# Layer 1's input groups in a two-layer adaLN transformer kernel: normalised one slot later and transposed in mid-slot; joined epsilon and power steps; no carrier copies

## What is computed

```
h = _layernorm(x) * (1 + ca) + sa;  x = x + ga * attention(h)
h = _layernorm(x) * (1 + cb) + sb;  x = x + gb * ffn(h)
```

## Time and profile before

| | us |
|---|---|
| median of 3 runs | 736.52 |
| the profiled execution's own time | 740.21 |
| its span, first to last instruction | 738.4 |
| PE busy (88%) | 647.3 |
| DVE busy (69%) | 511.4 |
| ACT busy (43%) | 319.5 |
| POOL busy (30%) | 222.5 |
| PE idle until `xn` of L1320 was ready, whole span (13 times, at most 3.6) | 18.0 |
| DVE, L1320, 112 tiles | 41.4 |
| DVE, L1203, 98 copies | 15.0 |

### The profile page before, as it was taken

The page is one execution under the profiler, slowest core; times in us unless marked ns, Lnnn a source line. Parts: engine busy times, 40 slices in busy tenths (PEclk is TensorE's granted clock), DMA queues, the critical chain, the costliest instruction groups (busy, mean ns, idle before and its releaser), DMA issues.

```text
span 738.4 us, 11039 instructions
## 1 busy us (share of the span) xinstructions
PE 647.3 (88%) x3816; PEld 504.9 (68%) x3828; DVE 511.4 (69%) x1465; ACT 319.5 (43%) x644; POOL 222.5 (30%) x225
## 2 busy tenths in 40 slices
PE   5889799988777999988889989958889998799997
PEld 4456687877556778775678777846677786576674
DVE  5957598696768667726669777596865754876665
ACT  1133344445234454543344444523445453554453
POOL 3333654343545211004455435253421102000000
PEclk9989999999879999999999999978999999999999
DMA  8400000000000000000000000000000000000001
GB/s 262 110 0 1 2 1 1 1 0 1 1 0 1 1 1 1 1 1 1 1 1 1 1 1 2 1 1 0 1 1 1 1 1 1 0 16 29 14 19 40
DMA packets 12078, 9.64 MB, mean 13 GB/s; under 512 B 1708, under 2 KB 10744, under 8 KB 12024
## 3 DMA queue, kind: packets, MB, share of 16 engines
q1 hardware_dynamic: 12024, 8.94, 4.1%
HBM read 6.84 MB, written 2.10 MB: 12 GB/s over the span
## 4 chain that ended last, share of the span: by engine, by line
PE 69%; DVE 18%; ACT 5%; POOL 4%; issue 4%; DMA 1%; SPq 0%; ACTq 0%; POOLq 0%
PE ps L777 14%; PE ps L647 12%; PE ps L755 8%; PE ps L606 5%; DVE xn L1320 5%; PE ps L922 4%; PE ps L924 4%; PE ps L923 4%; PE ps L800 3%; PE ps L665 2%; PE ps L801 2%; PE ps L595 2%; PE ps L816 2%; DVE row_max L1357 1%; PE ps L601 1%
## 5 line engine op out<-in xcount | busy, mean ns | idle before, releaser
L1083 ACT ACTIVATE probsT<-ps 128x512 f32<-128x512 f32 (+3 forms) x160 | 85.2, 533 | 180.4 <-PE ps L755 180.4
L777 PE MATMUL ps<-v_sb,probsT 128*128 128x129 f32 (+1 forms) x1148 | 157.1, 280 | 3.7 <-ACT probsT L1085 3.7
L777 PEld LDWEIGHTS ps<-v_sb,probsT 128*128 128x128 f32 (+1 forms) x1148 | 141.5, 191 | 10.6 <-ACT probsT L1085 5.5
L1357 DVE TENSOR_REDUCE row_max<-ps 128x1 f32<-128x512 f32 (+2 forms) x144 | 87.6, 619 | 48.3 <-PE ps L647 18.1
L755 PE MATMUL ps<-ident,probs 128*128 128x128 f32 (+1 forms) x574 | 95.7, 285 | 16.7 <-ACT probsT L1083 6.0
L755 PEld LDWEIGHTS ps<-ident,probs 128*128 128x128 f32 (+1 forms) x574 | 67.5, 143 | 49.0 <-issue 45.3
L1057 ACT ACTIVATE probs<-ps,neg_max 128x512 f32<-128x512 f32 (+7 forms) x158 | 92.8, 618 | 16.9 <-DVE neg_max L1364 16.0
L473 POOL TENSOR_TENSOR rstd<-veps,half 128x4 f32<-128x4 f32 x34 | 34.2, 1012 | 154.1 <-DVE veps L1211 153.9
L501 POOL TENSOR_TENSOR hq<-ha,hp 128x352 f32<-128x352 f32 x32 | 29.9, 934 | 139.5 <-DVE hp L1398 139.5
L647 PE MATMUL ps<-k_high,q_high 128*128 128x512 f32 (+4 forms) x112 | 46.0, 411 | 0.6 <-ACT probs L1005 0.6
L1152 ACT ACTIVATE probs<-ps 128x512 f32<-128x512 f32 x40 | 24.0, 599 | 44.7 <-PE ps L924 44.7
(11 more groups left out here) (240 smaller groups left out, 1380.8 us busy)
## 6 DMA issues: line engine op xcount, KB each, us to landing
out<-x_sb SPq DMA_DIRECT2D x8, 256.0 KB, 2.3
x_sb<-in_L_attn_x SPq DMA_DIRECT2D x2, 512.0 KB, 5.3
hT_all<-in_L_wmod SPq DMA_DIRECT2D x2, 384.0 KB
rope_cos<-table_cos SPq DMA_DIRECT2D x1, 768.0 KB, 7.5
rope_sin<-table_sin SPq DMA_DIRECT2D x1, 768.0 KB, 9.1
rope_cos<-table_cos SPq DMA_DIRECT2D x1, 256.0 KB, 4.1
rope_sin<-table_sin SPq DMA_DIRECT2D x1, 256.0 KB, 5.1
moe_raw<-in_L_ffn_expert_gate_w SPq DMA_DIRECT2D x1, 256.0 KB, 4.2
```

Source lines behind the costliest of these rows:

```text
L777: mm = pe.matmul(bank(OUT_AT, 0, V_W), probsT[0:size, n % 4, k * P:(k + 1) * P], v_sb[0:size, j, :], start=(c == 0 and k == 0), stop=(c == ...
L1083: ins = act.activation(probsT[:, n % 4, 0:full], bank(TURN, 0, full), ACT.Copy)
L1357: ins = dve.tensor_reduce(dst, ps[:, start:start + width], AX.X, ALU.max, negate=single)
```

## The change

1. norm2 leaves `input_turns` and `normalise_in_slot`. Group g is normalised in slot 4g + 13 instead of 4g + 12, on DVE between the first maximum and `combine` (`normalise_keys`), and transposed in mid-slot on PE, behind the second scores; ACT copies it behind `copy_hq`.
2. Where norm1 or norm3 and norm2 end in one slot (slots 11, 15, 19, 23), eight `bn_aggr` follow each other, and one epsilon and one power of 128x8 replace two of 128x4. The semaphores per kind are merged accordingly.
3. `carry_wait` is gone: the waits stand on the instructions behind it.

```diff
-    firsts = (("fp4_in", FFN_LAG), ("norm2", DOWN_LAG + GROUP + 1), ("norm3", TILES + GROUP + 2))
+    firsts = (("fp4_in", FFN_LAG), ("norm3", TILES + GROUP + 2))
...
+def key_group(slot):
+
+    return group_at(slot, DOWN_LAG + GROUP + 1)
...
-                    if at(NORM1_SLOT) is not None:
-                        rsqrt(0, at(NORM1_SLOT))
-                    if at(NORM2_SLOT) is not None:
-                        rsqrt(1, at(NORM2_SLOT))
+                    if s % GROUP == GROUP - 1:
+                        rsqrt(0, 1 + (at(NORM2_SLOT) is not None), b * 2 * GROUPS + s // GROUP + 1)
...
                         if c + 1 < following:
                             scores(s + 1, c + 1)
+                        if c == 0 and key_group(s) is not None:
+                            turn_group(("norm2", key_group(s)))
...
                             copy_hq(s - DOWN_LAG)
+                        if c == 0 and key_group(s) is not None:
+                            copy_group(("norm2", key_group(s)))
...
-            def carry_wait():
-
-                dve.tensor_copy(tick[:], ones[:, 0:1])
-
-            def send_statistics(kind, link):
-
-                carry_wait()
-                for k in range(GROUP):
-                    ins = dve.bn_aggr(mv[:, kind, k, :], bn[:, kind, k, :])
+            def send_statistics(kind, kinds, link):
+
+                for n in range(kind, kind + kinds):
+                    for k in range(GROUP):
+                        ins = dve.bn_aggr(mv[:, n, k, :], bn[:, n, k, :])
                 link(ins)
-                dve.tensor_scalar(veps[:, kind, :], mv[:, kind, :, 1], LN_EPS, None, ALU.add).then_inc(var_ready[kind], 1)
+                rows = slice(kind, kind + kinds)
+                dve.tensor_scalar(veps[:, rows, :], mv[:, rows, :, 1], LN_EPS, None, ALU.add).then_inc(var_ready[kind // 2], 1)
...
-                    if at(NORM2_SLOT) is not None:
-                        normalise(1, at(NORM2_SLOT), at(NORM2_SLOT)).then_inc(xn_ready, 1)
...
+                def normalise_keys(g):
+
+                    normalise(1, GROUPS // 2 + g, g).then_inc(xn_ready, 1)
...
                     if following:
                         maximum(s + 1, 0)
+                    if key_group(s) is not None:
+                        normalise_keys(key_group(s))
```

More of the change, by code:

```diff
@@ L140, in turn_order @@
                 order.append(("hq", s - DOWN_LAG))
+            if c == 0 and key_group(s) is not None:
+                order.append(("norm2", key_group(s)))
     return order + [("norm3", GROUPS - 1)]
@@ L154 @@
 ROPE_SUMS = 2 * (GROUPS - 1)
-NORM_GROUPS = (2 * GROUPS, GROUPS, GROUPS)
+NORM_GROUPS = (2 * GROUPS, 2 * GROUPS, GROUPS)
 parts_before, MAX_PARTS = before(lambda l, i: len(score_chunks(l, i)) if len(score_chunks(l, i)) > 1 else 0)
-STEPS_PER_BATCH = 185
+STEPS_PER_BATCH = 177
 def build(nc, x, cos, sin, wq, wk, wv, w_gate, w_up, w_down, c0, wmod0, qk, ov, gate_w, lb_bias,
@@ L204, in build @@
         unpick = sb("unpick", [P, PAIRS, P], BF16)
-        half = sb("half", [P, GROUP])
+        half = sb("half", [P, 2, GROUP])
         priority = sb("priority", [P, EXPERTS])
@@ L326, in build @@
         tanh_ready = sem("tanh_ready")
-        var_ready = [sem(f"var_ready_{k}") for k in range(3)]
-        rstd_ready = [sem(f"rstd_ready_{k}") for k in range(3)]
+        var_ready = [sem(f"var_ready_{k}") for k in ("inner", "first")]
+        rstd_ready = [sem(f"rstd_ready_{k}") for k in ("inner", "first")]
         xn1_ready = sem("xn1_ready")
@@ L468, in _, with rsqrt @@
             pool.tensor_copy(ident_b[:], ident[:]).then_inc(consts, 1)
[L470 to L476, removed]
+            def rsqrt(kind, kinds, n):
+                rows = slice(kind, kind + kinds)
+                pool.wait_ge(var_ready[kind // 2], n)
+                pool.tensor_tensor(rstd[:, rows, :], veps[:, rows, :], half[:, 0:kinds, :],
+                                   ALU.pow).then_inc(rstd_ready[kind // 2], 1)
+            rsqrt(2, 1, 1)
+            rsqrt(2, 1, 2)
             pool.wait_ge(fp4_scaled, 1)
@@ L484, in _ @@
             for b in range(BATCH):
-                def rsqrt(kind, n):
-                    rsqrt_at(kind, b * NORM_GROUPS[kind] + n + 1)
                 def modulate_1(g):
@@ L554, in _ @@
                     if early_group(s, NORM0_SLOT) is not None:
-                        rsqrt(2, early_group(s, NORM0_SLOT))
+                        rsqrt(2, 1, b * GROUPS + early_group(s, NORM0_SLOT) + 1)
                     if s in (NEXT_SLOT - 2, NEXT_SLOT):
-                        rsqrt(2, GROUPS + (s == NEXT_SLOT))
-                    if at(NORM1_SLOT) is not None:
-                        rsqrt(0, at(NORM1_SLOT))
-                    if at(NORM2_SLOT) is not None:
-                        rsqrt(1, at(NORM2_SLOT))
+                        rsqrt(2, 1, (b + 1) * GROUPS + (s == NEXT_SLOT) + 1)
+                    if s % GROUP == GROUP - 1:
+                        rsqrt(0, 1 + (at(NORM2_SLOT) is not None), b * 2 * GROUPS + s // GROUP + 1)
                     if at(NORM2_SLOT + 2) is not None:
                         keys_low(at(NORM2_SLOT + 2))
-                    if at(NORM3_SLOT) is not None:
-                        rsqrt(0, GROUPS + at(NORM3_SLOT))
                     if at(FP4_SLOT) is not None:
@@ L1221, in first_statistics @@
                 link(ins)
-                send_statistics(2, link)
+                send_statistics(2, 1, link)
             def first_normalise(b, batch, g):
-                dve.wait_ge(rstd_ready[2], (b + 1) * GROUPS + g + 1)
+                dve.wait_ge(rstd_ready[1], (b + 1) * GROUPS + g + 1)
                 for t in range(GROUP):
@@ L1306, in x_tile, with statistics @@
                     return x_sb[:, bass.ds(b * TILES + t, n), :].rearrange("p t d -> p (t d)")
[L1308 to L1314, removed]
+                def statistics(kind, t):
+                    return dve.bn_stats(bn[:, kind, t % GROUP, :], x_tile(t))
                 def normalise(kind, n, g):
-                    dve.wait_ge(rstd_ready[kind], b * NORM_GROUPS[kind] + n + 1)
+                    dve.wait_ge(rstd_ready[kind // 2], b * NORM_GROUPS[kind] + n + 1)
                     for t in range(GROUP):
@@ L1346, in norm_0_statistics @@
                 def norm_0_statistics(g):
-                    statistics(2, range(g * GROUP, (g + 1) * GROUP))
+                    for t in range(g * GROUP, (g + 1) * GROUP):
+                        ins = statistics(2, t)
+                    link(ins)
+                    send_statistics(2, 1, link)
                 def maximum(s, c):
@@ L1377, in finish @@
                     dve.wait_ge(x_attn, b * SLOTS + s + 1)
-                    carry_wait()
-                    statistics(0, [i])
+                    ins = statistics(0, i)
                     if ffn_tile(s, DOWN_LAG) is not None:
-                        statistics(1, [s - DOWN_LAG])
+                        ins = statistics(1, s - DOWN_LAG)
+                    if s % GROUP == GROUP - 1:
+                        link(ins)
+                        send_statistics(0, 1 + (ffn_tile(s, DOWN_LAG) is not None), link)
                 def quantise(a, m, src, n_blocks, scales, last_wait):
```

## The result

The kernel with the change took **760.21 us** (median of 4 runs, 758.13 to 762.10) against 736.65 us before (4 runs): ratio 1.0313, 95% interval 1.0273 to 1.0352. It is slower by 23.6 us, where 14.2 us were forecast, and lies above the range of 735 to 757.

The account below looks back on a forecast made before the run. PE's work, 69% of the chain, was taken to set the time except where PE waits for DVE. Terms of 5.8 + 1.1 + 0 + 1.0 - 1.8 + 1.0 = 7.1 us a batch, 14.2 for two, gave 750.7 us, range 735 to 757.

Parts of the forecast that it names:

- The sign and the mechanism: Slower: DVE reaches norm2's tiles late, beside POOL's work, so PE stands in mid-slot; chance of slower 0.77.
- slot 13 to L757: Slot 13: PE waits for late tiles, then bare ACT copies, and goes on later: +5.8 us a batch, undisturbed +1.7.
- slot 17: Tiles beside `xq_scaled` free `TURN` at 209.8 for next slot's L696, which ran at 208.66: +1.1 us, undisturbed -2.9.
- slot 25, to L757: Slot 25, POOL quiet: tiles can no longer be done while PE is in the slot before: +1.0 us.
- The DVE chain of slot 13: DVE's maximum done at 158.1, `xq_scaled` on POOL from 157.6, four tiles ready at 161.8.
- the clock's term: Slot 13: PE's stand three times as long, restart at lower clock: +1.0 us a batch, between 0 and 3.
- a deeper clock loss: Rival: PE stays at 1.2 GHz for the rest of slots 13 and 21: +3 a batch, 755 us; chance 0.14.
- My 0 for slot 21: Slot 21: tiles beside `hq_scaled`, transposition and copies end at 239.4, before 239.39: 0 us, undisturbed -0.5.
- The savings: Joined statistics and no copies: 0.8 off in slots 19 and 23 each, 0.2 elsewhere: -1.8 us a batch.
- The tiles are not held up: Rival: POOL and DVE interleave better than in slot 12: -2.5 a batch, 731.5 us; chance 0.13.
- The waits simply go: Rival: PE's waits in slots 13, 17, 21 and 25 vanish, 7.8 us a batch: 721 us; chance 0.04.

Follow-up runs that it names:

- the first experiment: Kernel before plus only the joined statistics and missing copies, norm2 left where it was: 733.27 us (10 runs) against 736.82, ratio 0.9951; again 734.17 us, ratio 0.9960.
- the run with early tiles: Changed kernel with norm2's four tiles normalised in slot 12 as before, PE still transposing them in mid-slot: 733.17 us (10 runs), ratio 0.9940 to the kernel before.

## Why the prediction was wrong in size

**The sign and the mechanism were right.** The table has the steps: slot 13 to L757 6.07 against 5.8; slot 17 1.1 as forecast, by cancellation as forecast (L698 doesn't wait for POOL now); slot 25, to L757, 1.0 as forecast. The DVE chain of slot 13 came within 0.1 us, less the 1.01: maximum done at 158.2 (158.1), POOL from 157.7 (157.6), last tile at 161.75 (161.8). `quantise_h` in slot 12 took 1.56 us longer beside the modulation, up to the start of `finish`, where I took 1.5. The 0.3 us that slot 13 lay above its term are a transposition at the lower clock, 1.11 us where 0.73 stood.

**The step that failed is the clock's term.** I charged +1.0 a batch, between 0 and 3, by a row of four turned probabilities at 1.2 GHz behind a stand of 2 us. Measured are 2.72 behind slot 13 and 1.6 behind slot 25, 4.3 in the first batch and 4.1 in the second: 3.3 and 3.1 more, 6.4 of the 9.4 us by which the forecast was short. I had named that "a deeper clock loss" and priced it at +3 with chance 0.14; it was this rival, and larger. Two errors are in it. I priced the restart by one row, and not by all that PE does until the clock is back (the clock is down from 158 to 171 us in slot 13, where before it was some 3 us, and PE works from 162.81 on). And I gave slot 25 nothing, since its waits are short: 0.67 and 1.63 us, one behind the other, were followed by over 2 us at 0.50. The run with matmuls in the wait bears this out: in slots 13 and 25 it gets 3.3 us back in the first batch and 4.5 in the second.

**Second, the base.** I added differences to the median as if the profiled execution were a usual one. It was not: its slot 21 had a stretch at 0.50 that took 1.6 us a batch. My 0 for slot 21 holds within that execution and is about 1.6 a batch too low against one without the stretch; whether a usual execution has it isn't shown. As the execution after also lay above its median, 3.6 - 1.9 = 1.7 us of the 9.4 are from the base. The setup and first slots give 1.0, which isn't shown to be the change's, and the other terms together 0.3. I had also said that a difference of 1.5 us can be told from none. The executions of before range from 730.86 to 742.08 us, and the intervals of four experiments are 5 to 6 us to either side.

**The savings** were right in sum: 1.8 us a batch on record, 1.8 by the first experiment's medians, though its interval is wide. They were wrong in place. In slot 23, where I took off 0.8, only 0.2 came. DVE's busy time did not drop by 15 us, only by 7.4 in the first experiment (504.0 us): the instruction behind a copy starts before the copy ends (a copy of 0.15 us at 140.98, the next at 141.06). In the kernel after the drop is gone again (511.0), as tiles and `quantise_h` beside POOL last longer.

**The rivals.** "The tiles are not held up" is contradicted by 3.64 and 3.77 us, and by the run with POOL held back even its premise would not have been enough: 754.61, where it said 731.5. That rival took DVE to be in time once undisturbed; it was not, by 5.26 us. "The waits simply go" holds for the run with early tiles, where they do go, and still the time stays at 733: what bounds slots 17 and 18 is then POOL's `xq`.

## What to carry to other kernels

Before moving a step behind other work on an engine, write down when that engine gets there, and compare it with when the consumer asks; this loss could be read from the trace of before. A wait on TensorE costs more than itself: behind one of 7.79 us the lower clock took another 2.72, and behind two short ones 1.6. So price all of TensorE's work until the clock is back, and look for stretches at the lower clock in a profiled execution that lies above its median before using it as the base. Where VectorE and GpSimd alternate, put what the critical engine waits for ahead of what starts GpSimd; here that was worth 6 us.

## What was unexpected on the hardware

- Two short waits in a row (0.67 and 1.63 us) had over 2 us at 1.2 GHz behind them, but the 1.54 and 1.63 us of slot 21 had not: the clock stayed at 1.00 there. In the kernel with nothing but the move the same two waits of slot 21 did have them, as its stretch shows:

```profile
248.00:250.00 2.00, 2.00 (x11) 2.00 (x11) 1.38 (x4) 0.75 (x2) 0.44 (x1) 0.50 0.03 8
```

So the lengths of the waits alone don't decide it, and no run tells what does.
- POOL's power of 128x8 took 1.65 us where 128x4 takes 1.01, as the source line's row of the kernel after shows (min, median, max in ns):

```profile
L481 POOL TENSOR_TENSOR rstd<-veps,half x26: 1006/1018/1647, 10.9 to 636.5; 128x4 f32<-128x4 f32 x18, 128x8 f32<-128x8 f32 x8
```

- A SCALAR_TENSOR_TENSOR of `quantise_h` took 1.34 us beside POOL's modulation and 0.53 without it.
